# Bilinear feature interaction in fp32: scores in pairs on TensorE, the four-row stores on GpSimd's queue, other slot counts

## What is computed

```python
bilinear = jnp.einsum('bie,ied->bid', feature, weight)   # feature (2048, 200, 64), weight (200, 64, 64)
out = jnp.einsum('bid,bjd->bij', bilinear, feature)      # (2048, 200, 200)
```

## Time and profile before

| | |
|---|---|
| median of 3 runs | 1574.05 us (1573.21 to 1574.11) |
| the profiled execution: its own time | 1573.6 us |
| the profiled execution: span from first to last instruction | 1571.8 us |
| TensorE matmul busy | 1525.3 us (97% of the span), granted clock 0.996 on average |
| VectorE busy | 1145.3 us (73%) |
| ScalarE busy | 928.2 us (59%) |
| DMA: bytes, rate | 438.51 MB, 279 GB/s over the span |

### The profile page before, as it was taken

The page is one execution under the profiler, slowest core; times in us unless marked ns, Lnnn a source line. Parts: engine busy times, 40 slices in busy tenths (PEclk is TensorE's granted clock), DMA queues, the critical chain, the costliest instruction groups (busy, mean ns, idle before and its releaser), DMA issues.

```text
span 1571.8 us, 40835 instructions
## 1 busy us (share of the span) xinstructions
PE 1525.3 (97%) x16192; PEld 1209.0 (77%) x16192; DVE 1145.3 (73%) x2048; ACT 928.2 (59%) x1313; POOL 0.7 (0%) x6
## 2 busy tenths in 40 slices
PE   8999999999999999999999999999999999999974
PEld 6888778877788777887778877788777887788753
DVE  0567777777777778678787687777777777786896
ACT  5666556655566655665556655566555665556532
POOL 0000000000000000000000000000000000000000
PEclk9999999999999999999999999999999999999998
DMA  9788999889989999989999899899999989999788
GB/s 234 226 270 267 297 295 282 280 268 293 296 275 288 281 293 283 292 275 277 288 289 292 274 281 296 275 289 280 290 290 283 286 273 290 288 280 289 239 266 248
DMA packets 294235, 438.51 MB, mean 279 GB/s; under 512 B 38049, under 2 KB 242849, under 8 KB 294049
## 3 DMA queue, kind: packets, MB, share of 16 engines
q1 hardware_dynamic: 294048, 435.92, 89.8%
HBM read 108.13 MB, written 327.68 MB: 277 GB/s over the span
## 4 chain that ended last, share of the span: by engine, by line
PE 88%; DVE 8%; issue 2%; DMA 1%; SPq 0%; ACT 0%; DVEq 0%
PE ps L219 49%; PE bp L203 24%; PE tp L187 14%; DVE staging L250 4%; DVE win L298 2%; DVE win L305 1%; PE ps L203 1%; PE ps L187 1%; DMA x<-feature_dram 0%; DMA out_dram<-staging 0%; DVE win L306 0%; SPq L138 0%; SPq L131 0%; ACT staging L250 0%; ACT bl L272 0%
## 5 line engine op out<-in xcount | busy, mean ns | idle before, releaser
L219 PE MATMUL ps<-win,bl 64*100 64x200 f32 x8192 | 932.3, 354 | 24.1 <-DVE staging L250 23.9
L219 PEld LDWEIGHTS ps<-win,bl 64*100 64x100 f32 x8192 | 699.7, 207 | 167.6 <-issue 164.7
L250 DVE COPY staging<-ps 100x800 f32<-100x800 f32 x512 | 505.8, 988 | 326.7 <-PE ps L219 324.6
L272 ACT COPY bl<-bp 128x512 f32<-128x512 f32 x384 | 322.3, 839 | 449.7 <-PE bp L203 449.7
L250 ACT COPY staging<-ps 100x800 f32<-100x800 f32 x512 | 423.1, 826 | 164.9 <-PE ps L219 162.9
L203 PE MATMUL bp<-xt,w 64*64 64x128 f32 x6144 | 419.7, 276 | 0.0
L203 PEld LDWEIGHTS bp<-xt,w 64*64 64x64 f32 x6144 | 326.8, 133 | 83.5 <-ACT xt L263 78.7
L298 DVE COPY win<-xt 128x400 f32<-128x400 f32 x512 | 276.7, 541 | 63.4 <-ACT xt L263 47.5
L187 PE MATMUL tp<-ident,x 128*128 128x128 f32 x1536 | 252.8, 287 | 5.9 <-DMA x<-feature_dram 5.9
L187 PEld LDWEIGHTS tp<-ident,x 128*128 128x128 f32 x1536 | 161.6, 141 | 89.3 <-issue 89.1
L263 ACT COPY xt<-tp 128x512 f32<-128x512 f32 x384 | 226.6, 590 | 5.3 <-PE tp L187 5.3
(11 more groups left out here) (4 smaller groups left out, 0.4 us busy)
## 6 DMA issues: line engine op xcount, KB each, us to landing
out_dram<-staging SPq DMA_DIRECT2D x1024, 300.0 KB, 4.1
x<-feature_dram SPq DMA_DIRECT2D x400, 256.0 KB, 4.1
out_dram<-staging SPq DMA_DIRECT2D x512, 25.0 KB
w<-weight_dram SPq DMA_DIRECT2D x24, 128.0 KB, 5.6
w<-weight_dram SPq DMA_DIRECT2D x2, 64.0 KB, 4.4
```

What stands on the lines that cost most here:

```text
L219: last = nc.tensor.matmul(ps[s % TILES][0:FH, h, F * b:F * (b + 1)], rows_of_bl(n, R * k + PB * i + b)[64 * h:64 * h + 64], win[64 * h:64 ...
L250: copy(staging[:, slot, :, :, :].rearrange("p b h j -> p h b j"), ps[s % TILES][0:FH, :, 0:PB * F].rearrange("p h (b j) -> p h b j", j=F)) ...
L272: nc.scalar.copy(group_of_bl(n, t), bilinear_tile(n, t).rearrange("p (c b) -> p c b", c=C)).then_inc(bl_stored, 1)
```

## The change

Five things are changed at once. On TensorE the second set of a quad now comes before the transposes, so that the two sets stand together and transposes and weighing follow each other. The four-row stores leave SyncE's queue for GpSimd's, in the same order among themselves, each behind a wait for both sets. `staging` grows from 12 sets to 16, `x` shrinks from 6 slots to 4 and `win` from 4 slots to 3. ScalarE's copy of `bp` to `bl` for odd blocks writes in the order of memory (4 neighbours, then the next sample) and reads PSUM with a step, where it read PSUM in order and wrote each number 512 bytes from the last. The reserve for GpSimd's DMA descriptors grows from 256 to 2048 bytes.

```diff
-    XSLOTS = 6
+    XSLOTS = 4
     TILES = 3
-    OSLOTS = 12
-    WSLOTS = 4
+    OSLOTS = 16
+    WSLOTS = 3
...
         def group_of_bl(n, t):
             if n % 2 == 0:
                 return bl[:, C * t:C * (t + 1), :]
-            return bl[:, :, C * t:C * (t + 1)].rearrange("p b c -> p c b")
+            return bl[:, :, C * t:C * (t + 1)]
...
-                if s % 2:
-                    wait_staged(sp, s - 1)
-                    sp.dma_start(out_v[FA:FH, PB * (s - 1):PB * (s + 1), :],
-                                 staging[FA:FH, slot - 1:slot + 1].rearrange("p s b h j -> p (s b) (h j)")
-                                 ).then_inc(rest_written[slot // 2], 16)
...
+            def store_rest(s):
+                slot = s % OSLOTS
+                wait_staged(pool, s - 1)
+                wait_staged(pool, s)
+                nc.gpsimd.dma_start(out_v[FA:FH, PB * (s - 1):PB * (s + 1), :],
+                                    staging[FA:FH, slot - 1:slot + 1].rearrange("p s b h j -> p (s b) (h j)")
+                                    ).then_inc(rest_written[slot // 2], 16)
+
+            for s in range(1, BLOCKS * SETS_B, 2):
+                store_rest(s)
...
                 for k in range(QUADS):
                     scores(n, k, 0)
+                    scores(n, k, 1)
                     if k in transposed_at and (n + 1) * NG + transposed_at[k] < BLOCKS * NG:
                         transposes((n + 1) * NG + transposed_at[k])
-                    scores(n, k, 1)
                     if k in weighed_at and n + 1 < BLOCKS:
                         bilinear(n + 1, weighed_at[k])
...
-                nc.scalar.copy(group_of_bl(n, t), bilinear_tile(n, t).rearrange("p (c b) -> p c b", c=C)
+                cells = "p (c b) -> p c b" if n % 2 == 0 else "p (c b) -> p b c"
+                nc.scalar.copy(group_of_bl(n, t), bilinear_tile(n, t).rearrange(cells, c=C)
                                ).then_inc(bl_stored, 1)
...
-    nc = bacc.Bacc("TRN2", target_bir_lowering=False, num_devices=1, dynamic_dma_scratch_size=256)
+    nc = bacc.Bacc("TRN2", target_bir_lowering=False, num_devices=1, dynamic_dma_scratch_size=2048)
```

More of the change, by code:

```diff
@@ L41, in feature_interaction @@
     assert 2 * E == 128 and B % NB == 0 and FH % C == 0 and NG <= QUADS and R == 2 * PB
-    assert PB * F <= 512 and C * NB == 512 and OSLOTS % 2 == 0
+    assert PB * F <= 512 and C * NB == 512 and OSLOTS % 2 == 0 and (BLOCKS * SETS_B) % OSLOTS == 0
     feature_v = feature.rearrange("b f e -> b (f e)")
```

## The result

The changed kernel takes 1516.6 us (median of 4 runs, 1514.0 to 1519.7) against 1573.7 (4 runs, 1573.2 to 1574.1): a ratio of 0.964, 95% interval 0.963 to 0.965. The forecast was 1517.

A forecast was written before the change was run, and what follows sets the result against it. TensorE was taken to bound fifteen blocks and VectorE the last. The terms summed as 1573.6 - 76 + 22 + 2 - 8 + 4 = 1517.6, given as 1517 us; own bounds 1502 to 1532, range 1500 to 1545.

The forecast's parts named there:

- TensorE's order: Quads with both kinds of work, blocks 0 to 14: pairing sets saves 0.24 us (even) or 0.18 (odd) each, 76 us.
- Three windows: At 15 block ends TensorE waits for VectorE's rounds, some 1.5 us more each: 22 us given back, bounds 0 and 34.
- Four x slots: Loads of x stay hidden in the blocks and come a little late in the opening: 2 us lost, between 0 and 9.
- the lead of 9.4 us against 8.6 at worst: In the blocks, three full quads of 9.4 us cover VectorE's copy, SyncE's issues and a landing, 6.3 to 8.6 us.
- The four-row stores, at the end: Off SyncE's queue, the span ends near 5 us behind VectorE instead of 13.7: 8 us saved, bounds 0 and 9.
- SyncE keeps up with two store issues per round: In the tail, with two store issues per 2.24 us round, SyncE no longer falls some ten microseconds behind VectorE.
- The four-row stores, in the blocks: Leaving SyncE one issue per quad is worth nothing in the blocks, as SyncE ends no wait of TensorE today.
- Sixteen staging sets: Staging for the copies out: worth nothing by themselves, since in the blocks no copy waits for a store.
- VectorE and GpSimd: VectorE's fills slowed by GpSimd's descriptor writing, 0.05 us on each of 85 rounds: 4 us lost, between 0 and 31.
- The rival in which GpSimd's stores are held: At the handover in VectorE's round, GpSimd's stores are held so long they set the pace: 1580 to 1700 us, chance 0.05.
- The rival of the transfers' limit: In the blocks, 27.0 MB each at 294 GB/s becomes the bound; if 285 were the cap, 1560 us; chance 0.05.

The follow-up runs named there:

- the better version: The changed kernel with the four-row stores on ScalarE's queue two quads late, six x slots, four windows and fourteen staging sets: 1496.2 us, ratio 0.951.

## Why the prediction was right, and where it was not

- **TensorE's order** (76 us): right in size and mechanism. The quads took 3.15 and 3.26 us, and where nothing else was in the way the order gave 78, the shorter end included.
- **Three windows** (22 us, waits at 15 block ends): the mechanism and the place are in the timeline; alone the change cost 24.7. But the term can't be read off the final sum: with the fourth window back, and four staging sets fewer, the time stayed at 1519, and TensorE waited for x instead, 29.1 us where the changed kernel waits 7.6.
- **Four x slots** (2 us, hidden in the blocks "barely at the worst"): the place in the opening was right, the first set starts at 51.5 instead of 50.3 us. In the blocks wrong: 9 us alone at the old order, 12 at the new one beside four windows. The step that failed is the lead of 9.4 us against 8.6 at worst: it put SyncE's issues at 2.2 us together, but the issue of a 300 KB store alone goes from 0.32 to over 2 us. Since the landings stayed under 6.4, the issues are what is left to explain it, which is argued. In the changed kernel the loss is small, for a reason that stays open (the next point); waits for x in 50 to 1430 us sum to 4.8 us at the weight load and 1.9 at the matmul.
- **Both kinds of slots against the rest: the luck.** Without the 22 + 2 us for windows and x slots the sum is 1573.6 - 76 - 8 + 4 = 1493.6; the run with all old slots took 1507.0, 13 more. Going on to the new slots cost 1516.6 - 1507.0 = 9.6 us, 14 less than the 24 forecast. The two errors cancel. Their place is in the traces: against the run with the old slots, TensorE's waits for x inside the blocks fall from 12.3 us to 1.9 in the changed kernel, and the end behind VectorE's last copy from 12.3 us to 8.2, together the size of what is missing from the 24 (single executions: that of the old slots, 1512.2 us, lies 5 us above its median). So the terms are not independent, and the sum added them as if they were. Whether it is TensorE's pause at each block end that lets the loads catch up, or the sixteen staging sets, no run separates. On ScalarE's queue the same step from old slots (with fourteen staging sets) costs 14.5.
- **The four-row stores, at the end** (8 us): 5.5. The span ends 8.2 us behind VectorE's last copy instead of 13.7. The step that failed is that SyncE keeps up with two store issues per round: it issues until 1510.7 us, 4.0 behind VectorE, and the landing comes on top. Nor is the 5.5 the queue's alone: with these stores back on SyncE the end is 10.9 us long, and with GpSimd's queue and the old slots 12.3.
- **The four-row stores, in the blocks** (nothing, "SyncE doesn't end any wait of TensorE today"): this step is wrong, and the largest error of the prediction. It holds at the old pace, where the queue alone changes nothing. At the new one it is worth 1546.2 - 1516.6 = 30 us. The error didn't reach the sum, because the change has both parts together: the sum took the order's 76 us whole, and SyncE's queue with all its stores does not allow them. Whoever had made the order's change alone on this working would have expected 1498 and found 1536.
- **Sixteen staging sets** (nothing, "in the blocks no copy waits for a store"): true at the old pace. At the new one, with twelve sets, ScalarE's copies wait for stores 91.9 us in the run with the order alone and 20.2 us (15 times) in the one with the old slots, and never in the changed kernel. No run changes this count alone, so its price is open.
- **VectorE and GpSimd** (4 us, 0.05 on each of 85 rounds): 4.9 us up to VectorE's last copy, 0.058 on the one fill. The rival in which GpSimd's stores are held had its place right and its price far off: GpSimd's issue is 0.57 us at the median and 0.81 at most, and its stores land after 4.6 us at the median, where SyncE's take 4.7. The page SBUF — State Buffer of the Trainium skill, section A bandwidth-pool intuition that's wrong, gives 620 ns for such a DMA alone and 3100 ns beside a VectorE copy; nothing of that size is seen here. A slower fill beside GpSimd's stores is what the same page's section Who interferes with whom, with its rule of a shared port, would lead one to look for, but it is 58 ns and on one of two fills; that the port causes it is not shown.
- **The rival of the transfers' limit** was given 0.05 on the ground that one window had 296 GB/s, and as a cap at 285 it did not come: the changed kernel holds 296 for a thousand microseconds and the better version 298. But the ground was too simple. What was late was x behind the stores of one queue, at 291 GB/s in the run with the order alone and so below the rate of that window; the rate of all transfers is no measure of whether one queue keeps up.

## What to carry to other kernels

A queue that ends no wait today can be the next bound at once: when an edit speeds up the bound engine by 5%, work out for each queue and for the transfers what they must carry at the new pace, and don't take a rate seen for a short while as proof that every queue keeps up. The length of a DMA issue can be a wait in disguise: here the same 300 KB store took 0.83 us at the median, and 0.32 with 2% less data behind it. And a sum that comes out right proves none of its terms: here two errors of 13 and 14 us cancelled, so undo each part, and undo parts together, before believing a price.

## What was not expected of the hardware

- A group of sets between other work costs TensorE 0.68 us per set and besides, once per group, 0.17 to 0.18 in odd blocks and 0.26 to 0.31 in even ones; weighing takes 1.02 us behind transposes and behind scores alike, so pairing the sets pays nothing back there.
- One small store of 25 KB per quad, moved from SyncE's queue to another, was worth 30 us (2%) at 290 GB/s and nothing at 279.
- ScalarE's queue took these stores at 0.26 us each and left VectorE's fills alone; GpSimd's took 0.57 us each and lengthened one of two fills from 367 to 425 ns.
- ScalarE's copy from PSUM takes 0.59 us when it writes four neighbours at a time and reads with a step of 512 bytes, and 1.05 us when it reads in order and writes each number 512 bytes on the earlier trace rows: the step costs at the writing end alone.
